# Group norm with a second constant matrix: the deviation of a channel's mean from TensorE, and a normalisation without a shift

## What is computed

```python
def _gn(v, G=32, eps=1e-05):
    B_, C_, H_, W_ = v.shape
    g = v.reshape(B_, G, C_ // G, H_, W_)
    m = jnp.mean(g, axis=(2, 3, 4), keepdims=True)
    s = jnp.var(g, axis=(2, 3, 4), keepdims=True)
    return ((g - m) / jnp.sqrt(s + eps)).reshape(v.shape)
...
x = x + _L0_conv_ref(_gn(x), L0_conv_w_off, L0_conv_b_off, L0_conv_w_conv)
x = x + _L1_conv_ref(_gn(x), L1_conv_W, L1_conv_b)
```

## Time and profile before

| | |
|---|---|
| median of 3 runs | 104.27 us (103.85 to 104.47) |
| span of the profiled execution, first to last instruction | 102.7 us; its own total is not shown |
| PE busy | 88.0 us (86%), 705 instructions |
| DVE busy | 63.1 us (61%), 136 instructions |
| ACT busy | 43.5 us (42%), 88 instructions |
| POOL busy | 28.4 us (28%), 31 instructions |
| group-mean products L372 | 5, recorded as 10 passes |

### The profile page before, as it was taken

The page is one execution under the profiler, slowest core; times in us unless marked ns, Lnnn a source line. Parts: engine busy times, 40 slices in busy tenths (PEclk is TensorE's granted clock), DMA queues, the critical chain, the costliest instruction groups (busy, mean ns, idle before and its releaser), DMA issues.

```text
span 102.7 us, 1892 instructions
## 1 busy us (share of the span) xinstructions
PE 88.0 (86%) x705; PEld 62.9 (61%) x705; DVE 63.1 (61%) x136; ACT 43.5 (42%) x88; POOL 28.4 (28%) x31
## 2 busy tenths in 40 slices
PE   5999994579998699999989999993999998999600
PEld 4655973368675388766668876662677655675200
DVE  1334239994388936699994669993396470738400
ACT  3203022645578605664940566494056573015100
POOL 7020016910019400209830020987002025020000
PEclk9999999999999999999999999999999999999975
DMA  2840000000000000000001000000000000010020
GB/s 49 248 121 16 10 0 0 0 6 0 0 3 0 6 0 0 0 0 6 3 0 51 0 6 0 0 0 0 32 19 6 0 0 0 0 51 0 0 67 0
DMA packets 2906, 1.80 MB, mean 18 GB/s; under 512 B 1561, under 2 KB 2841, under 8 KB 2895
## 3 DMA queue, kind: packets, MB, share of 16 engines
q1 hardware_dynamic: 2271, 1.36, 4.5%
q10 hardware_dynamic: 624, 0.31, 1.1%
HBM read 1.14 MB, written 0.52 MB: 16 GB/s over the span
## 4 chain that ended last, share of the span: by engine, by line
PE 48%; issue 22%; POOL 12%; DVE 9%; ACT 2%; POOLq 1%; ACTq 0%
PE prep_ps L383 9%; PE ring L414 9%; POOL sim L324 8%; PE samp_ps L433 8%; PE out_ps L346 6%; PE out_ps L444 4%; DVE hats L812 3%; PE att_ps L352 2%; PE att_ps L513 2%; POOL S L310 2%; PE ring L501 1%; DVE S L833 1%; DVE hats L800 1%; POOL rstd L303 1%; PE ring L491 1%
## 5 line engine op out<-in xcount | busy, mean ns | idle before, releaser
L414 PE MATMUL ring<-table,S 128*128 128x128 f32 x144 | 19.6, 279 | 2.2 <-issue 1.9
L650 ACT COPY ST<-ring 128x512 f32<-128x512 f32 x32 | 17.5, 595 | 8.1 <-PE ring L414 7.9
L414 PEld LDWEIGHTS ring<-table,S 128*128 128x128 f32 x144 | 15.5, 141 | 7.4 <-issue 6.0
L433 PE MATMUL samp_ps<-ST,xT 128*64 128x320 f32 (+1 forms) x128 | 19.1, 418 | 0.3 <-ACT sampled L659 0.3
L833 DVE TENSOR_TENSOR S<-hats 128x1152 f32<-128x1152 f32 x12 | 18.1, 1523 | 0.8 <-POOL hats L316 0.8
L659 ACT COPY sampled<-samp_ps 128x640 f32<-128x640 f32 x16 | 11.1, 692 | 9.2 <-PE samp_ps L433 9.1
L303 POOL TENSOR_TENSOR rstd<-var,table 128x1 f32<-128x1 f32 (+1 forms) x6 | 3.7, 622 | 36.2 <-DVE var L766 36.2
L433 PEld LDWEIGHTS samp_ps<-ST,xT 128*64 128x64 f32 x128 | 9.9, 136 | 5.5 <-issue 3.0
L310 POOL TENSOR_TENSOR S<-hats 128x1152 f32<-128x1152 f32 x4 | 11.0, 2743 | 0.3
L383 PE MATMUL prep_ps<-gpad,woff_T 128*64 128x128 f32 x144 | 10.1, 302 | 0.6 <-DVE gpad L785 0.6
L383 PEld LDWEIGHTS prep_ps<-gpad,woff_T 128*64 128x64 f32 x144 | 9.5, 155 | 1.5 <-DVE gpad L785 0.9
(11 more groups left out here) (94 smaller groups left out, 98.4 us busy)
## 6 DMA issues: line engine op xcount, KB each, us to landing
x_sb<-x SPq DMA_DIRECT2D x4, 128.0 KB, 2.8
out<-y_sb SPq DMA_DIRECT2D x4, 128.0 KB, 1.7
table<-consts ACTq DMA_DIRECT2D x1, 130.0 KB, 3.1
woff_nat<-w_off SPq DMA_DIRECT2D x1, 121.5 KB
table<-consts ACTq DMA_DIRECT2D x1, 92.0 KB, 3.7
wconv_nat<-w_conv ACTq DMA_DIRECT2D x1, 80.0 KB, 4.2
wconv_nat<-w_conv SPq DMA_DIRECT2D x1, 80.0 KB, 2.6
boff_col<-b_off SPq DMA_DIRECT2D x4, 0.1 KB
```

Source lines behind the costliest of these rows:

```text
L414: mm = pe.transpose(ring[i % RING][:, 128 * n:128 * n + 128], S[:, k % S_BUFS, s, 128 * w:128 * w + 128], ident)
L433: mm = pe.matmul(samp_ps[64 * h:64 * h + 64, a, 64 * lo:64 * hi], xT[:, k % 2, w if general else 2 * j + a, C * b:C * b + C], ST[:, k % 2, ...
L650: nc.scalar.copy(dst, ring[i % RING][:]).then_inc(ring_act, 1)
```

## The change

A second constant matrix `deviation` = `average` - identity joins the table, so that PE gives for each partition the group's mean minus the channel's own mean. `group_means` issues two products in place of one, and `group_ps` holds three columns for each pair in place of two. `group_variance` no longer forms the difference on DVE. It adds epsilon while it copies the averaged variance out, and for a single pair squares the deviation and adds in one operation; for three pairs it takes two. The normalisation is now (x - mean) x rstd, where it was x x rstd + shift; it waits for `rstd` and not for the shift. The shift is still made for ACT's copy in group norm 1 (`shift_of`); in group norm 2 it is gone.

```diff
@@ constants
+    deviation = average - ident
-    return np.concatenate([ident, average, power, ones, cy, cy_window, cx], 1).astype(np.float32)
+    return np.concatenate([ident, average, deviation, power, ones, cy, cy_window, cx], 1).astype(np.float32)
@@ run_pairs
-        gmv = sb("gmv", [128, 2, PAIRS, 2])
-        gdiff = sb("gdiff", [128, 2, PAIRS])
+        gmv = sb("gmv", [128, 2, PAIRS, 3])
+        gvar_eps = sb("gvar_eps", [128, 2, PAIRS])
...
-        minus_half = table[:, 256:256 + PAIRS]
-        early = 256 + PAIRS
+        deviation = table[:, 256:384]
+        minus_half = table[:, 384:384 + PAIRS]
+        early = 384 + PAIRS
@@ group_ps
-            return ps[:, 0:2 * n].rearrange("p (k s) -> p k s", s=2)
+            return ps[:, 0:3 * n].rearrange("p (k s) -> p k s", s=3)
@@ group_means
-                pe.matmul(group_ps(part), average, mv[:, i, lo:hi, :], start=True, stop=True).then_inc(gn_group[i], 1)
+                pe.matmul(group_ps(part)[:, :, 0:2], average, mv[:, i, lo:hi, :], start=True, stop=True)
+                pe.matmul(group_ps(part)[:, :, 2], deviation, mv[:, i, lo:hi, 0], start=True, stop=True).then_inc(gn_group[i], 1)
@@ group_variance
                 nc.vector.tensor_copy(gmv[:, i, lo:hi, :], group_ps(part)).then_inc(gn_own[i], 1)
-                nc.vector.tensor_tensor(gdiff[:, i, lo:hi], group_ps(part)[:, :, 0], mv[:, i, lo:hi, 0],
-                                        ALU.subtract).then_inc(gn_own[i], 1)
-                dve.wait_ge(gn_own[i], own[i] + 2)
-                nc.vector.tensor_tensor(var[:, i, lo:hi], gdiff[:, i, lo:hi], gdiff[:, i, lo:hi], ALU.mult).then_inc(gn_own[i], 1)
-                own[i] += 3
+                nc.vector.tensor_scalar(gvar_eps[:, i, lo:hi], group_ps(part)[:, :, 1], EPS_GN, None, ALU.add).then_inc(gn_own[i], 1)
+                own[i] += 2
                 dve.wait_ge(gn_own[i], own[i])
-                nc.vector.scalar_tensor_tensor(out=var[:, i, lo:hi], in0=gmv[:, i, lo:hi, 1], scalar=EPS_GN,
-                                               in1=var[:, i, lo:hi], op0=ALU.add, op1=ALU.add).then_inc(gn_var[i], 1)
-
-            def scale_and_shift(part):
+                if hi - lo == 1:
+                    nc.vector.scalar_tensor_tensor(out=var[:, i, lo:hi], in0=gmv[:, i, lo:hi, 2], scalar=gmv[:, i, lo, 2:3],
+                                                   in1=gvar_eps[:, i, lo:hi], op0=ALU.mult, op1=ALU.add).then_inc(gn_var[i], 1)
+                else:
+                    nc.vector.tensor_tensor(var[:, i, lo:hi], gmv[:, i, lo:hi, 2], gmv[:, i, lo:hi, 2], ALU.mult).then_inc(gn_own[i], 1)
+                    own[i] += 1
+                    dve.wait_ge(gn_own[i], own[i])
+                    nc.vector.tensor_tensor(var[:, i, lo:hi], var[:, i, lo:hi], gvar_eps[:, i, lo:hi], ALU.add).then_inc(gn_var[i], 1)
+
+            def shift_of(part):
...
-                dve.wait_ge(gn_shift[i], n + 1)
@@ normalise
-                nc.vector.tensor_scalar(dst, src, rstd[:, i, k:k + 1], shift[:, i, k:k + 1], ALU.mult, ALU.add).then_inc(g_ready[i], 1)
+                dve.wait_ge(gn_rstd[i], k + 1 if i == 1 else min(k, 1) + 1)
+                nc.vector.tensor_scalar(dst, src, gmv[:, i, k, 0:1], rstd[:, i, k:k + 1], ALU.subtract, ALU.mult).then_inc(g_ready[i], 1)
@@ DVE, opening
             group_variance(GN1_FIRST)
-            scale_and_shift(GN1_FIRST)
             normalise(0, 0)
+            shift_of(GN1_FIRST)
...
-            scale_and_shift(GN1_REST)
+            shift_of(GN1_REST)
             normalise(0, 1)
@@ DVE, loop
-                    scale_and_shift(gn2(k - 1))
                     normalise(1, k - 1)
```

## The result

The changed kernel is slower: median 104.72 us of 18 runs (103.44 to 105.70), beside 103.82 us of 18 runs of the kernel before (102.45 to 104.57). The ratio is 1.0127 with a 95% interval of 1.0086 to 1.0168. On another chip, beside the experiments, it was 1.0067 (1.0016 to 1.0117), with medians 104.96 and 103.93. The ratios leave out disturbed runs, those more than 1.5% over the fastest of their kernel. Single runs of one kernel scatter by up to 3.4 us here, so medians are given too, and the stages of the traces carry the argument.

What follows compares the result with a forecast made beforehand. PE's own stream was taken to bound the middle, DVE's chain the last pair. The terms 0.15+0.04-0.11+0.66-0.13 = +0.61 us took the median 104.27 to 104.9, range 104.1 to 105.9.

Steps and rivals of the forecast that it cites:

- Part 5: Turns 1 to 3: PE's stream is the path, so three second products cost their pitch, +0.66 us; lower end 0.36.
- the chain's 0.12: Middle: the cost in us that the profile's chain credits to the existing group-mean product; taken as lower end per product.
- cheap pairs: Rival, middle and tail: a second product hides like the first, 0.12 each; sum +0.18, 104.45 us; chance 0.18.
- a middle that PE doesn't bound: Rival, turns 1 to 3: slack takes in the three pairs, -0.05 remains, 104.2 us; chance 0.10.
- Part 6: Last pair: DVE's chain is the path; PE's product adds 0.25, DVE saves 0.19 twice; together -0.13 us.
- The warm-up products did not hold it: Last pair, the contrary case: 17 warm-up products free PE only at 91.35, so the tail gains nothing (+0.04 us).
- Part 3: First norm, pairs 1 to 3: DVE's last operation ends later and the hat distances start at 15.01, +0.04 us.
- Part 4: Before the second convolution: the normalisation no longer waits for the shift and starts 0.08 behind it, -0.11 us.
- Part 2: Opening: the second product costs its loads' pitch, 0.28, which the clock change cuts to 0.15 us; upper end 0.41.
- The discount for a rise that keeps its time: Opening: work pushed across a clock change at fixed time costs 1.97/3.60 of what it did, so 0.28 becomes 0.15.
- Part 1: Opening: the first table load grows by 64 KB but still lands before it is needed, 0; upper end 0.26 us.
- The rate did rise at another time: Rival, opening: the clock rises earlier, before the first convolution, -1.0 us in all, 103.2; chance 0.08.

Runs made afterwards that it cites:

- e1: The changed kernel once more, beside the experiments on their chip: 104.96 us against 103.93 of the kernel before, ratio 1.0067.
- e7: The changed kernel with the deviation product issued twice in turns 1 to 3: 105.61 us, +1.38 against the kernel before, ratio 1.0180.
- e5: The kernel before with four more products, results unread, at the first group means: 106.30 us, +2.07, ratio 1.0196.
- e12: The kernel before with 128 unread columns more in the first table load, second execution: 104.59 us, +0.30, ratio 1.0029.
- e8: The kernel before with only the normalisation changed (subtract mean, multiply by rstd, no wait for a shift): 103.65 us against 104.23, ratio 0.9965.
- e11: The kernel before with 128 unread columns more in the second table load: 104.06 us, 0.00 against the kernel before, ratio 0.9995.
- e10: The changed kernel without the opening's second product, the matrix still in the first load: 104.99 us, +0.93 against the kernel before, ratio 1.0138.
- e9: The kernel before once more, unchanged, as a kernel of its own: 104.14 us against 104.06, +0.08.
- e6: The kernel before with 128 unread columns more in the first table load, first execution: 104.79 us, +0.56, ratio 1.0092.

## Why the prediction was right, and where it was short

The direction held, and so did the mechanism of the middle and of the last turn: the forecast of 104.9 was 0.6 over the median known then, and the change costs 0.9 to 1.0 by medians (by the ratios 1.27%, 1.3 us, and 0.67%, 0.7 us). That 104.9 lies within 0.2 of the measured 104.72 is partly luck: the 104.27 of three runs stood 0.45 over the median of 18, and the sum stood 0.3 under the change. The terms, each against its stage:

- **Part 5, the middle, +0.66:** 0.67, and the same again when doubled. Taking the pitch rather than the chain's 0.12 was right. The Trainium skill's 0.107 us per load of 128 columns ("TensorE: Matmul & The Clock Gate", LDWEIGHTS) gives an estimate of 0.21 per product, and the trace agrees in the middle: 0.22. It does not agree in an opening at the lower level, where a product takes 0.43. The rivals of cheap pairs and of a middle that PE doesn't bound are both out.
- **Part 6, the last turn, -0.13:** -0.11. The warm-up products did not hold it. The fused operation's own 0.22 in place of 0.16 was not in the working.
- **Part 3, the rest of the first norm, +0.04:** +0.05.
- **Part 4, no wait for the shift, -0.11:** -0.28, and this term stood too small. The start came 0.12 earlier as worked out. What I left out is who else starts there: POOL's mask began 0.03 us before the normalisation, and now it comes second. The pitch of 0.07 without the wait (0.19 with it) speaks again, for operations this small, against what "VectorE: DVE Perf Modes" (section "The DRAIN you can't avoid") in the Trainium skill says, that a semaphore between chained operations costs nothing extra.
- **Part 2, the opening's product, +0.15:** this is the step that failed. In an opening at the lower level the pitch is 0.43, that of the matmuls, which I had as the upper end, and not the 0.28 of the loads. In one at the upper level it is 0.21, and the claim that PE works on behind it without a pause is wrong: in e1 and e7 PE waited for `woff_nat`, which hid the product. The discount for a rise that keeps its time stays open: e5's total speaks against it, e5's trace for it. Its size was off in any case, since the 3.60 us of the first convolution hold passes of both levels; wholly at the lower level it took 4.1 (e12).
- **Part 1, the load, 0:** 0.18 at least. I asked when the table would land and not what else lands beside it; the image on the other queue came later, and the statistics wait for that. `woff_nat` came later too.

With the product in full it is 0.18+0.43+0.05-0.28+0.67-0.11 = 0.94, and 0.51 where it is hidden; I had 0.61. The middle and the later stages are shown to some 0.03 us; what the opening costs depends on the execution. The rate did rise at another time: 2.84 us from the first convolution to the bias in one trace of the changed kernel and 3.89 in the other. Kernels without the product scatter as much (2.90 in e8, 4.15 in e11), so nothing shows this as an effect of the change. It is also why the first pair of traces misleads: the changed kernel's span is 102.6 us and that of before 102.7. For the view that shows the change at all, one has to cut the traces at instructions that stand behind the opening.

Not settled: e10's total, what part of an opening product reaches the end, and how much of the difference between 1.27%, 0.67% and the 0.94 us (0.9%) is scatter.

## What to carry to other kernels

A tiny product on TensorE costs about 0.22 us here wherever TensorE's stream is the path, and 0.43 at the lower level; DVE can form the same difference in 0.07 beside operations that it issues anyway. In each stage, move work only to the engine that waits there. When single runs scatter more than the effect, cut the traces at fixed instructions: a stage repeated here within 0.03 us while the totals scattered by 3. And when a stage and the total disagree, as for e5, say so and follow the work to the last instruction.

## What the runs showed of the hardware that I had not expected

- **TensorE's rate in the opening differs from execution to execution of one kernel.** e12 and e9 have the same instructions on PE. These are the granted-clock lines of their pages (tenths of full speed in 40 slices), first e12:

```profile
PEclk9995579599999999999999999999999999999985
```

and e9:

```profile
PEclk9999999999999999999999999999999999999998
```

  In e12 the clock is granted in full for 7.7 us, then falls to the lower level, 1.2 GHz, goes up and down once more, and stays at 2.4 GHz from about 21 us on. In e9 no fall is recorded. Yet e9's opening was the slower one: the group mean's passes start 0.20 apart (0.10 in e12), and its convolution ran passes of 421 ns until about 12.3 us. So the clock line alone does not tell the rate of the opening; the distance between passes does. The passes of the first convolution took 421 ns in e12, as those before the change of rate in the kernel before:

```profile
L383 PE MATMUL prep_ps<-gpad,woff_T x16: 421/421/421, 12.1 to 13.6; 128*64 128x128 f32 x16
```

  PE was busy with warm-up products and transposes all through, but for short waits at the group mean (0.27 us for `mv` and 0.17 for `woff_nat` in e12). First mean to bias took 8.52 us in e6 and 9.69 in e12, which are one kernel.
- **The stretch behind the last instruction of DVE takes 4.7 to 6.7 us**, and no engine works in it; it holds the last write-out. It took 6.58 and 5.33 us in two executions of one kernel.
- **A 0.1 us earlier start can save 0.14 us of duration.** Of DVE's normalisation and POOL's mask, the one that began second took longer: 0.55 in place of 0.41 for DVE, 0.61 in place of 0.43 for POOL. All 14 traces agree to 0.01: six with the old order, eight with the new.
